# Gathering a kernel's guard values with TensorE and VectorE instead of GpSimd, and moving a wait for the last store

## The reference

```python
scores = einsum('bhid,bhjd->bhij', Q, K) / sqrt(32)        # Q, K, V = layernorm(x) @ W.T + b
scores = where(causal_mask, -inf, scores) + decay          # decay = -(i - j)
out = einsum('bhij,bhjd->bhid', softmax(scores), V) @ Wo.T + bo
x = x + layernorm(out)
xq = quantize_activations(layernorm(x) @ H)                # 4 bits
x = x + layernorm(einsum('bsi,oi->bso', xq, ternary(weight)))
```

## Time and profile before

| | |
|---|---|
| median of 3 runs | 1153.63 us (1151.25 to 1153.74) |
| the profiled execution | 1153.24 us |
| its span, first to last instruction | 1151.6 us |
| PE, DVE, ACT, POOL busy | 94%, 86%, 61%, 51% of the span |
| granted clock of PE, mean | 0.978 of 2.4 GHz |

### The profile page before, as it was taken

The page is one execution under the profiler, slowest core; times in us unless marked ns, Lnnn a source line. Parts: engine busy times, 40 slices in busy tenths (PEclk is TensorE's granted clock), DMA queues, the critical chain, the costliest instruction groups (busy, mean ns, idle before and its releaser), DMA issues.

```text
span 1151.6 us, 44392 instructions
## 1 busy us (share of the span) xinstructions
PE 1083.2 (94%) x18369; PEld 726.2 (63%) x18400; DVE 985.4 (86%) x2572; ACT 708.0 (61%) x1493; POOL 589.7 (51%) x723
## 2 busy tenths in 40 slices
PE   4899999999999999999999999999999999999852
PEld 3566666676666676676666676666667676667421
DVE  5859998889988888899888889988888998887684
ACT  5455666766576676656666665666676656666542
POOL 1334555555554655555555565555655655465421
PEclk9999999999999999999999999999999999999876
DMA  9647666655566675566667565556765665665311
GB/s 276 140 108 146 142 151 164 144 145 137 139 127 152 163 152 141 140 144 132 145 153 168 126 156 132 132 139 156 166 146 139 139 138 131 154 140 131 93 49 44
DMA packets 204830, 161.78 MB, mean 140 GB/s; under 512 B 150449, under 2 KB 150705, under 8 KB 204529
## 3 DMA queue, kind: packets, MB, share of 16 engines
q1 hardware_dynamic: 199888, 141.86, 55.1%
q0 software_dynamic: 4736, 17.04, 4.2%
HBM read 40.87 MB, written 16.78 MB: 50 GB/s over the span
## 4 chain that ended last, share of the span: by engine, by line
PE 72%; DVE 20%; issue 3%; DMA 2%; ACT 1%; SPq 1%; POOLq 1%; POOL 0%; DVEq 0%; ACTq 0%
PE f_job L1392 47%; PE f_st L1493 6%; PE f_o L1512 5%; PE f_o L1515 3%; PE f_job L1568 3%; DVE f_bst L1028 2%; PE f_job L1468 2%; DVE f_rmax L991 2%; PE f_job L1550 2%; DVE f_stage L977 2%; DVE f_inverse L1020 1%; DVE f_x L1072 1%; PE f_job L1558 1%; DVE f_o L1018 1%; DVE f_z L1130 1%
## 5 line engine op out<-in xcount | busy, mean ns | idle before, releaser
L508 POOL TENSOR_SCALAR_AFFINE_SELECT f_PT<-f_PT 64x512 f32<-64x512 f32 (+1 forms) x256 | 205.3, 819 | 144.3 <-ACT f_PT L674 100.0
L523 POOL TENSOR_TENSOR f_square<-f_stage 128x512 bf16<-128x512 f16 x128 | 130.9, 1045 | 88.1 <-ACT f_stage L652 74.2
L1392 PE MATMUL f_job<-f_xTh,f_wqh 128*128 128x256 f16 x512 | 140.8, 275 | 17.8 <-DMA f_xTl<-f_xl 14.7
L514 POOL TENSOR_TENSOR f_OTl<-f_o,f_OTh 128x256 f16<-128x256 f32 x127 | 84.0, 668 | 135.4 <-ACT f_OTh L692 135.3
L652 ACT ACTIVATE f_stage<-f_job,f_bias 128x256 f16<-128x256 f32 x256 | 106.4, 467 | 74.2 <-PE f_job L1392 66.9
L1392 PE MATMUL f_job<-f_xTl,f_wqh 128*128 128x256 f16 x512 | 140.1, 274 | 0.0
L1392 PE MATMUL f_job<-f_xTh,f_wql 128*128 128x256 f16 x512 | 140.1, 274 | 0.0
L1392 PE MATMUL f_job<-f_xTh,f_wkh 128*128 128x256 f16 x512 | 139.9, 273 | 0.0
L1392 PE MATMUL f_job<-f_xTh,f_wkl 128*128 128x256 f16 x512 | 139.8, 273 | 0.0
L1392 PE MATMUL f_job<-f_xTl,f_wkh 128*128 128x256 f16 x512 | 139.7, 273 | 0.0
L977 DVE SCALAR_TENSOR_TENSOR f_stage<-f_job,f_bias,f_stage 128x256 f16<-128x256 f32 x256 | 111.1, 477 | 29.5 <-ACT f_stage L652 28.9
(11 more groups left out here) (199 smaller groups left out, 2957.0 us busy)
## 6 DMA issues: line engine op xcount, KB each, us to landing
f_stacks<-f_stage SPq DMA_DIRECT2D x380, 128.0 KB
f_xin<-x SPq DMA_DIRECT2D x33, 512.0 KB, 4.0
f_x<-x SPq DMA_DIRECT2D x31, 512.0 KB, 4.6
out<-f_z POOLq DMA_DIRECT2D x31, 512.0 KB, 3.3
f_Vmix<-f_V SPq DMA_DIRECT2D x32, 256.0 KB, 3.3
f_Vmix<-f_V SPq DMA_DIRECT2D x64, 128.0 KB, 3.3
f_stacks<-rows_const SPq DMA_DIRECT2D x3, 512.0 KB, 5.3
f_stacks<-wqT SPq DMA_DIRECT2D x2, 512.0 KB, 6.3
```

Source lines behind the costliest of these rows:

```text
L508: nc.gpsimd.affine_select(out=d, in_=d, compare_op=ALU.is_ge, fill=0.0, base=odd * SUB, pattern=[[0, 4], [0, TP], [1, SUB]], channel_multi ...
L514: nc.gpsimd.tensor_tensor(OT[s % 2][1][:, g, :], o32[:, g % 2, :], OT[s % 2][0][:, g, :], ALU.subtract).then_inc(OTl_made, 1)
L523: nc.gpsimd.tensor_tensor(square[:, 2 * m + pair, :], h, h, ALU.mult).then_inc(squared, 1)
L1392: mm = pe.matmul(dst, lhs[a](c), rhs[b](c), start=(n == 0), stop=(n == 3 * KC - 1))
```

## The change

The all-reduce on POOL goes. PE transposes `guard` into 16 partitions x 128 values in PSUM (`turn_guards`), DVE takes the maximum of each row (`gather_guards`), PE transposes the 16 maxima back into one row (`turn_guards_back`), and `judge` copies that row out of PSUM before its five operations. `ident` gets a tile of its own, so that it lives to the end. SP's wait for the last stores is taken out of the block and put behind the barrier and behind the loads of the flag; for that the block is closed by hand within `fast_path`.

```diff
-        ident = x1[1][:, 0, 0:P]
+        ident_sb = sb("ident", [P, P], F32)
+        ident = ident_sb[:]
...
-        guard2 = sb("guard2", [P, 16], F32)
+        guard_top = sb("guard_top", [16, 1], F32)
+        guard_row = sb("guard_row", [1, 16], F32)
...
-        block = ctx.enter_context(nc.Block())
+        work = ctx.enter_context(ExitStack())
+        block = work.enter_context(nc.Block())
...
-            sp.wait_ge(last_out_done, 16 * TP)
...
-            def spread_guards():
-                pool.wait_ge(guard_step, 8)
-                nc.gpsimd.partition_all_reduce(guard2[:], guard[:], P, bass.bass_isa.ReduceOp.max)\
-                  .then_inc(guard_spread, 1)
...
             z_root(last)
-            spread_guards()
             pool.wait_ge(out_done, 16 * last)
...
+            def gather_guards():
+                dve.wait_ge(guard_turned, 1)
+                nc.vector.tensor_reduce(guard_top[:], ps_st[0][0:16, 0:P], AX_X, ALU.max).then_inc(guard_gathered, 1)
+
             def judge():
-                dve.wait_ge(guard_spread, 1)
+                dve.wait_ge(guard_turned, 2)
+                judged(nc.vector.tensor_scalar(guard_row[:], ps_st[0][0:1, P:P + 16], 1.0, None, ALU.mult))
                 dve.wait_ge(limits_made, len(LIMITS))
-                g1, passed = guard2[0:1, :], guard[0:1, :]
+                g1, passed = guard_row[:], guard[0:1, :]
...
             level_term(last)
+            gather_guards()
             scale_out(last, 0)
...
+            def turn_guards():
+                pe.wait_ge(expd, 8 * STEPS)
+                pe.wait_ge(guard_step, 8)
+                pe.transpose(ps_st[0][0:16, 0:P], guard[:], ident).then_inc(guard_turned, 1)
+
+            def turn_guards_back():
+                pe.wait_ge(guard_gathered, 1)
+                pe.transpose(ps_st[0][0:1, P:P + 16], guard_top[:], ident[0:16, 0:16]).then_inc(guard_turned, 1)
...
             turn_q(last, 1)
+            turn_guards()
             second(last, 0)
             second(last, 1)
+            turn_guards_back()
+
+        work.close()
+        flag = nc.values_load(flag_sb[:], min_val=0, max_val=1)
+        nc.sync.wait_ge(last_out_done, 16 * TP)
+        return flag
```

More of the change, by code:

```diff
@@ L257, in fast_path @@
         guard_step = sem("guard_step")
-        guard_spread = sem("guard_spread")
+        guard_turned = sem("guard_turned")
+        guard_gathered = sem("guard_gathered")
         limits_made = sem("limits_made")
@@ L2267 @@
     with nc.sbuf_tensor("flag", [1, 1], I32) as flag_sb:
-        fast_path(nc, *args, *fast_args, out, flag_sb)
-        flag = nc.values_load(flag_sb[:], min_val=0, max_val=1)
+        flag = fast_path(nc, *args, *fast_args, out, flag_sb)
         with nc.If(flag > 0):
```

## The result

| | before | after |
|---|---|---|
| median of 5 runs each | 1153.63 us (1151.25 to 1153.88) | 1146.98 us (1145.67 to 1149.33) |
| the profiled execution | 1153.24 us | 1145.91 us |
| its span | 1151.6 us | 1144.3 us |
| granted clock of PE, mean | 0.978 | 0.978 |

The ratio is 0.9949, with a 95% interval from 0.9937 to 0.9961: 5.9 us less (4.5 to 7.3). A second measurement of the same changed kernel gave 1147.97 us and 0.9954 (0.9937 to 0.9971). The forecast was 1148.3 us, 5.3 us less.

What follows compares the result with a forecast made beforehand. PE bounds the run (94% busy), but POOL holds its end: DVE's wait 4.02 plus POOL's drain past DVE's 1.83, minus copy 0.19, transpose 0.25, hop 0.05, gives 5.36 us less. Median 1153.63 becomes 1148.3 us, range 1146.2 to 1150.0.

Steps and rivals of the forecast that it cites:

- The wait for the all-reduce: DVE's idle time between the last residual and judging, while POOL sets up the all-reduce; 4.02 us would go.
- The first transpose: On PE between its last turn and the last products; all of it on the path, 0.25 us added.
- The wait ahead of it, the reduction, the turn back: PE's wait before the first transpose, DVE's row maximum (0.3 us), PE's transpose back behind the products; all claimed to cost nothing.
- The judging: DVE's operations after the last residual: six with the copy from PSUM, 1.09 us, starting 0.03 us after the residual.
- POOL's drain: At the block's end behind the last root; 0.17 to 3.03 us, taken as covered, over before DVE is done.
- The rival that the drain is long whatever stands ahead of it: POOL's 9.03 us belong to its drain, not the all-reduce; span 1151.9 us, no change; 4 in 100.
- SP's wait: SP's wait for the last stores; left in the block it would hold the barrier by some 0.8 us.
- The way out: From the end of the last drain through barrier, flag load and PE's branch to the span's end; 4.64 us, unchanged.
- The rival of a longer branch: PE's 3.75 us branch over the general path grows, at worst by as much again; 1.6 us gained; 3 in 100.
- The tile of the identity: Own tile for `ident`, 512 bytes a partition, moving later tiles; no added instruction, taken as costing nothing.
- The rival on the slower side: Moved tiles lengthen all 32 steps; at 0.3 us a step 1157.9 us; 5 in 100, 3 of them slower.
- the hop to POOL: From DVE's drain to POOL at the block's end barrier; 0.05 us added.

Runs made afterwards that it cites:

- e11: Kernel before with SP's wait moved behind the barrier and the last root on ACT, all-reduce kept on POOL behind the additions; 1150.29 us, one run.
- e4: Kernel before with SP's wait moved, last root on ACT, and the all-reduce ahead of the last additions for `out`; 1153.69 us, ratio 1.0009.
- e10: Changed kernel with eight small blocks of POOL fills, products, roots, loads or stores ahead of it; drains 0.14, 0.71, 2.98 us behind 1, 8, 36 loads.
- e5: Changed kernel with one useless root added at POOL's end, released by the last residual; 1150.03 us, one run.
- e6: Changed kernel with one useless addition at POOL's end, released by the last residual; 1148.35 us, one run.
- e1: Changed kernel with SP's wait for the last stores put back into the block; 1146.62 us, ratio 0.9945.
- e2: Kernel before with only SP's wait moved behind the barrier and the flag loads; 1152.25 us, ratio 0.9995.
- e9: Changed kernel with seven small blocks ahead of it, one useless POOL fill, addition, load or root in each; drains 34 to 43 ns, 138 behind the load.
- e3: Kernel before with only `ident` in a tile of its own; 1151.96 us, ratio 0.9997.
- e0: The changed kernel measured and profiled again, nothing altered; 1147.97 us, ratio 0.9954.
- e8: Changed kernel with guards judged before the last products, last root on ACT, and POOL's wait for `out` behind the barrier; 1147.05 us, ratio 0.9953.

## Why the prediction was right, point by point

- **The wait for the all-reduce** and the 6 us ahead of it: right. DVE's wait went (4.13 us against 4.02), and e11 and e4 show that they come with the all-reduce wherever it is put.
- **The first transpose**: 0.25 taken, 0.21 measured. It followed its neighbour at twice the float16 price alone; the 0.05 for a semaphore wasn't there. The Trainium skill's four passes for float32 (FP8 and Floating Point Precision, "TensorE Precision Notes") would have made 0.42 at this clock, an estimate; the trace disagrees.
- **The wait ahead of it, the reduction, the turn back**: right. PE had no idle time before L1578; the reduction took 0.28 us (0.3 taken) and left 1.43 us of DVE's wait; the turn back was done 5 us before its reader.
- **The judging**: six operations in 1.09 us (1138.38 to 1139.47), as taken. It started 0.08 us before the residual's end, not 0.03 after it, which is 0.1 us of the sum.
- **POOL's drain**: "covered" held, but by 0.5 us only. It ended 3.03 us after POOL's last operation, at the upper bound of the 0.17 to 3.03 given. The prediction had no reason for either bound; e10 gave one. The rival that the drain is long whatever stands ahead of it was right in part: 3.0 of the 9.03 us are the drain's, for its 36 transfers (e5, e6, e10), 6 are set-up and all-reduce.
- **SP's wait**: the mechanism was right, the size 1.1 us (e1) in place of 0.8. Without the first part it is worth nothing (e2).
- **The way out**: 4.64 us taken as before. Measured from DVE's drain PE's branch starts 0.87 us later, as it did from POOL's drain before (0.88 by the trace's finer times), and the branch was 3.65 us against 3.75. The rival of a longer branch didn't come in either profile of the changed kernel, but e1 (4.81) and e9 (5.26) show that the branch isn't of one length. The sum took its length over as fixed; a branch like theirs would have taken back 1.1 to 1.6 us of the gain, and that neither profile had one is luck.
- **The tile of the identity**: nothing that shows (e3), and the steps in the middle of the run are as before. The rival on the slower side didn't come.
- **The sum**: 5.36 us forecast, 5.7 shown in the two traces (5.4 and 5.8 from the start of the last turn, where the clock has its part), 5.9 (4.5 to 7.3) by the ratio. The 0.3 us that were missing lie in small terms of the same sign: DVE's wait 0.11, the branch 0.10, the hop to POOL 0.05, the transpose 0.04. The median fell by 6.65; what that is beyond 5.7 is less than the 1.2 us by which two profiles of the changed kernel differ where the last step begins.

## What to carry to other kernels

Look at the last microseconds apart from the averages: there an operation of 0.39 us cost 6, and hid that another engine's wait and POOL's own drain stood right behind it. This all-reduce cost its set-up wherever it stood, and in the one case tried the way back to ordinary work cost as much again, so look for both before it goes on a path that something waits for or in front of other GpSimd work; a reduction of a few columns over the partitions can go through PE and DVE, mostly in their gaps. And where two holds meet at one barrier, removing the one that ends first is worth nothing (e2), while removing the one that ends last gains only up to the next (e1): find the second in the profile before judging the first.

## What the runs showed of the hardware that was not expected

- POOL's drain at a block's end takes about 0.05 us and 0.081 us for each transfer issued from POOL's queue since its last drain, though all have landed (e10), and starts counting at the later of its own start (e0: 3.01 us from there) and the end of POOL's last operation (e5, e6). In e8, where POOL's last store was still under way, it ended 3.97 us after that store's issue, 1.0 us more than the rule gives; that is open.
- The way back from the all-reduce to ordinary operations of POOL took 6.9 us, with a MODIFY_POOL_CONFIG of its own at its start (e4).
- Small DVE operations on two SBUF inputs took 1.16 and 1.20 us beside POOL's additions, against 0.15 and 0.16 alone (e4). The Trainium skill, GPSIMD Engine Reference, "Key points", names contention of the two engines for DVE instructions with two SBUF inputs; the trace agrees. Of the one-input operations of the same chain only the first overlaps them, by 0.07 us, so nothing is shown of those.
- PE's branch over the general path took 3.46 to 4.15 us in twelve of the fourteen kernels, 4.81 in e1 and 5.26 in e9; the other engines' took 0.04 to 0.07. Its length goes with the packets of the queue called "instruction": within the branch one packet of 16 KB moves in the twelve and two in e1 and e9, and the branch ends 1.4 to 1.6 us after the last of them is over (1.95 in e1). Why there are two in these two kernels is open, and no run changed it on purpose.
